# A decoder layer on one core: the experts' up products as three products of rounded parts

## What is computed

```
scores = softmax(xt @ gate_w.T)                     # xt: 2048 x 128, 8 experts
idx = top_k(scores + gate_b, 2);  weights = scores[idx]
for each expert e:                                  # w1[e], w3[e]: 128 x 512, w2[e]: 256 x 128
    h = swiglu((xt @ w1[e] + b1[e]) * (xt @ w3[e] + b3[e]))
    routed += comb[:, e] * (h @ w2[e] + b2[e])      # comb is zero unless e was picked
shared = swiglu((xt @ sw1 + sb1) * (xt @ sw3 + sb3)) @ sw2 + sb2
out = layernorm(xt + routed + shared)
swiglu(x) = min(g, 7) * sigmoid(1.702 * min(g, 7)) * (clip(l, -7, 7) + 1),  g, l = even and odd columns
```

## Time and profile before

| | us |
|---|---|
| runs of the kernel before | 437.20, 444.21, 435.69; median 437.2 |
| the profiled execution, device time | 439.32 |
| its span, first to last instruction | 437.6 |
| attention slots 12 to 46 | 76 to 188 |
| attention slots 47 to 63 | 188 to 246 |
| tiles 0 to 7 with the last chains | 246 to 279 |
| tiles 8 on, with the last routing and padding | 279 to 321 |
| tiles at an even pace | 321 to 406 |
| sums and last norm | 406 to 438 |

### The profile page before, as it was taken

How to read it: one execution, slowest core, us unless ns; L and a number is a source line. 1 busy time by engine, 2 the same in 40 slices (tenths; PEclk the granted TensorE clock), 3 DMA queues, 4 the chain that set the end, 5 groups by cost and what they waited for, 6 DMA issues and landing times.

```text
span 437.6 us, 8506 instructions
## 1 busy us (share of the span) xinstructions
PE 355.7 (81%) x2402; PEld 231.0 (53%) x2415; DVE 280.9 (64%) x834; ACT 175.9 (40%) x498; POOL 192.0 (44%) x377
## 2 busy tenths in 40 slices
PE   2638588878987986987998599887989999999791
PEld 1223356656654764766667455444445555555450
DVE  3424257656877767686876876788566666666422
ACT  1211224433543432334444244434455556555404
POOL 9700014312211366531662344436775666656323
PEclk9999969979988788896989779999999999999896
DMA  4763734575617523130112000102211111110063
GB/s 100 167 184 94 214 90 111 181 225 153 186 66 219 181 81 87 32 103 28 41 52 97 2 18 18 50 13 79 76 54 50 45 44 44 42 45 30 19 199 96
DMA packets 53197, 39.56 MB, mean 90 GB/s; under 512 B 7623, under 2 KB 46632, under 8 KB 53147
## 3 DMA queue, kind: packets, MB, share of 16 engines
q1 hardware_dynamic: 50881, 34.33, 28.1%
q0 software_dynamic: 2272, 4.69, 3.2%
HBM read 26.05 MB, written 12.69 MB: 89 GB/s over the span
## 4 chain that ended last, share of the span: by engine, by line
PE 45%; DVE 23%; issue 8%; DMA 6%; POOL 6%; SPq 5%; ACT 5%; another core or an unknown queue 2%; ACTq 0%; POOLq 0%; DVEq 0%
PE pT L1468 6%; PE pS L1468 6%; PE pM L1479 3%; DVE negmax L921 3%; PE pM L1276 2%; PE pT L1445 2%; PE pT L1300 2%; PE pO L1459 2%; DVE PT L1052 2%; POOL rstd L602 2%; PE pS L1290 2%; PE pO L1313 2%; DMA X<-in_x 2%; PE pS L1469 1%
## 5 line engine op out<-in xcount | busy, mean ns | idle before, releaser
L700 POOL DMA_INDIRECT ys<-sim_rhs,row_dest x39 | 40.7, 1045 | 41.7 <-ACT sim_rhs L855 39.9
L921 DVE TENSOR_REDUCE negmax<-pS 128x4 f32<-128x512 f32 x64 | 43.2, 679 | 19.5 <-PE pS L1290 19.3
L755 ACT ACTIVATE PT<-pT 128x512 f32<-128x512 f32 x64 | 38.1, 595 | 43.9 <-PE pT L1300 43.0
L1290 PE MATMUL pS<-Kdiag,Qst 128*128 128x512 f32 x64 | 42.8, 678 | 13.4 <-DMA Qst<-parts_scr 12.9
L1468 PE MATMUL pT<-W,XH 128*128 (+1 forms) x94 | 51.1, 625 | 0.2 <-issue 0.2
L1468 PE MATMUL pS<-W,XH 128*128 (+1 forms) x94 | 49.0, 603 | 0.0
L1052 DVE TENSOR_TENSOR PT<-pT,PT 128x512 f32<-128x512 f32 x47 | 32.4, 690 | 24.6 <-PE pT L1469 11.4
L600 POOL TENSOR_SCALAR vareps<-meanvar 128x1 f32<-128x1 f32 x32 | 7.3, 227 | 88.9 <-DVE meanvar L950 88.7
L839 ACT COPY XH<-pO 128x384 f32<-128x384 f32 x47 | 22.5, 479 | 48.1 <-PE pO L1461 42.2
L1479 PEld LDWEIGHTS pM<-W,XH 128*128 128x128 f32 x188 | 28.0, 191 | 21.2 <-issue 17.5
L622 POOL DMA_INDIRECT xs<-X,slot x32 | 33.5, 1045 | 8.3 <-issue 6.0
(11 more groups left out here) (264 smaller groups left out, 834.0 us busy)
## 6 DMA issues: line engine op xcount, KB each, us to landing
parts_scr<-qk_hi SPq DMA_DIRECT2D x16, 256.0 KB, 2.9
W<-in_L_ffn_w SPq DMA_DIRECT2D x16, 256.0 KB, 3.2
Kdiag<-parts_scr SPq DMA_DIRECT2D x64, 48.0 KB
Qst<-parts_scr SPq DMA_DIRECT2D x32, 96.0 KB
Kst<-parts_scr SPq DMA_DIRECT2D x32, 96.0 KB
Qdiag<-parts_scr SPq DMA_DIRECT2D x64, 48.0 KB
sim_add<-xs SPq DMA_DIRECT2D x39, 65.0 KB
parts_scr<-qk_lo SPq DMA_DIRECT2D x8, 256.0 KB, 3.4
```

The lines of the kernel that those rows point to most:

```text
L700: pool.indirect_dma_start(ys.ap(), bass.IndirectOffsetOnAxis(ap=row_dest[:, k:k + 1], axis=0), YO[:, i % RING, :], None).then_inc(s_ysc[i ...
L755: act.activation(PT[:, u % 3, :], pT[:, 0, :], ACT.Exp, scale=SCALE).then_inc(p_sb, 1)
L921: dve.tensor_reduce(out=negmax[:, b % 2, HG * j:HG * (j + 1)], in_=pS[:, u % 2, :].rearrange("p (g k) -> p g k", g=HG), axis=AX.X, op=ALU.max,
L1290: pe.matmul(pS[:, u % 2, :], Qst[:, (b // 2) % 2, j, (b % 2) * P:(b % 2 + 1) * P], Kdiag[:, b % 2, j, :, :], start=True, stop=True).then_i ...
```

## The change

The 39 routed tiles no longer multiply float32 operands in the up products. A weight matrix w is split into an upper part rounded to float32r and a lower part, the rest rounded to float32r, and so is x; then x·w is computed as x_hi·w_hi + x_hi·w_lo + x_lo·w_hi, three float32r products. The shared expert's tiles keep float32.

The splitting of the 16 matrices (8 experts, w1 and w3) is a pipeline over slots 12 to 45, two slots a matrix, in four steps: SP loads the raw matrix into one of two buffers (slot 12+2k, after waiting for the store of matrix k-2 to land), ACT copies it rounded into W1 or W3 (next slot, at its end), POOL subtracts in place (the slot after, at its end), SP stores the lower part to a DRAM scratch (the slot after that). When the attention is done with `Kdiag` and `Qdiag`, their place takes the lower parts: 16 loads from the scratch in slots 54, 58, 60 and 64. The down weights come in slots 62 and 66. POOL no longer halves them; instead the row weight is halved, the b2 biases are doubled once (`twice`), and two ACT copies become multiplications by 0.5. In a tile, ACT makes x_hi after its copy to XH, and DVE x_lo between the clips and the gate. `hankel`, `flip`, `x2_of` and one `hidT` move from W1 and W3 to W2. Some semaphores are merged, so that POOL's bias step of slot 10 also waits for the two b_col loads.

```diff
-HALVE_SLOTS = {14: E, **{36 + e: e for e in range(E)}}
-UP_SLOTS = {**{15 + 4 * e: e for e in range(E - 2)}, 62: E - 2, 63: E - 1}
-DOWN_SLOTS = {13 + 4 * k: (2 * k, 2 * k + 1) for k in range(E // 2)}
+SPLIT_LOADS = {54: 0, 58: 1, 60: 2, 64: 3}
+SPLIT_SLOT = 12
+DOWN_SLOTS = {62: range(E // 2), 66: range(E // 2, E)}
...
+    up_scr = nc.dram_tensor("up_scr", (2 * E, P, I2), F32)
...
+        x_hi, x_lo = (t[:, 0, 0, :].rearrange("p (r n) -> p r n", r=2) for t in (Qst, Kst))
+        raw = [sb("raw", [P, I2])[:], W2[:, 3 * G4 * P:4 * G4 * P]]
+        W_lo = [t[:].rearrange("p k j g n -> p (k j g n)") for t in (Kdiag, Qdiag)]
...
+            def raw_weights(k):
+                if k >= 2:
+                    sp.wait_ge(s_w_copy[k % 2], 16 * (k // 2))
+                sp.dma_start(raw[k % 2], (w1, w3)[k // E][k % E]).then_inc(s_w_raw[k % 2], 16)
+
+            def store_lower(k):
+                sp.wait_ge(w_lo, k + 1)
+                sp.dma_start(up_scr.ap()[k], raw[k % 2]).then_inc(s_w_copy[k % 2], 16)
+
+            def load_lower(q):
+
+                sp.wait_ge(s_ps if q < 2 else sT_ps, U * (B - 1 + q % 2))
+                for r in range(2):
+                    sp.wait_ge(s_w_copy[r], 16 * E)
+                for k in range(4 * q, 4 * q + 4):
+                    sp.dma_start(split_of(k)[1].bitcast(F32), up_scr.ap()[k]).then_inc(s_w_lo, 16)
...
-                if n in UP_SLOTS:
-                    if n >= SHARED_SLOT + SHARED_SLOTS * SG:
-                        sp.wait_ge(f_ps, 9 * SG)
-                    up_weights(UP_SLOTS[n], s_w_up if UP_SLOTS[n] < E - 2 else s_w_last)
+                if split_step(n, 0) is not None:
+                    raw_weights(split_step(n, 0))
+                if split_step(n, 3) is not None:
+                    store_lower(split_step(n, 3))
...
-                    pool.tensor_scalar(W2[:, e * I:(e + 1) * I], W2[:, e * I:(e + 1) * I], 0.5, None, ALU.mult).then_inc(w2_half, 1)
+                if split_step(n, 2) is not None:
+                    k = split_step(n, 2)
+                    pool.wait_ge(w_hi, k + 1)
+                    pool.tensor_tensor(raw[k % 2].bitcast(F32R), raw[k % 2], split_of(k)[0].bitcast(F32),
+                                       ALU.subtract).then_inc(w_lo, 1)
...
+                if split_step(n, 1) is not None:
+                    k = split_step(n, 1)
+                    act.wait_ge(s_w_raw[k % 2], 16 * (k // 2 + 1))
+                    act.copy(split_of(k)[0], raw[k % 2]).then_inc(w_hi, 1)
...
                     act.copy(XH[:, p, :], pO[:, 0:3 * P]).then_inc(xh_sb, 1)
+                if NA <= m + 1 < NT:
+                    if m >= NA + 1:
+                        act.wait_ge(b_ps, m)
+                    act.wait_ge(xh_sb, m + 2)
+                    act.copy(x_hi[:, p, :], XH[:, p, 2 * P:3 * P]).then_inc(x_hi_sb, 1)
...
+                r = i + 2
+                if NA <= r < NT:
+                    if r >= NA + 2:
+                        dve.wait_ge(b_ps, r - 1)
+                    dve.wait_ge(x_hi_sb, r - NA + 1)
+                    dve.tensor_tensor(x_lo[:, 1 - p, :], XH[:, 1 - p, 2 * P:3 * P], x_hi[:, 1 - p, :].bitcast(F32),
+                                      ALU.subtract).then_inc(x_lo_sb, 1)
...
-                    pe.matmul(bank, XH[:, 1 - p, 2 * P:3 * P], W[:, bass.ds(e_up * I2, I2)], start=True, stop=False)
+                    if m < NA:
+                        pe.matmul(bank, XH[:, 1 - p, 2 * P:3 * P], (W1_shared, W3_shared)[k][:], start=True, stop=False)
+                    else:
+                        upper, lower = W[:, bass.ds(e_up * I2, I2)], W_lo[k][:, bass.ds(e_up * I2, I2)]
+                        if k == 0:
+                            pe.wait_ge(x_hi_sb, m - NA + 1)
+                        pe.matmul(bank, x_hi[:, 1 - p, :], upper, start=True, stop=False)
+                        pe.matmul(bank, x_hi[:, 1 - p, :], lower, start=False, stop=False)
+                        if k == 0:
+                            pe.wait_ge(x_lo_sb, m - NA + 1)
+                        pe.matmul(bank, x_lo[:, 1 - p, :], upper, start=False, stop=False)
```

More of the change, by code:

```diff
@@ L215, in decoder_layer @@
         hid = sb("hid", [P, 2, I])
-        hidT = [hid[:].rearrange("p k n -> p (k n)"), W1[:, (E - 2) * I2:(E - 1) * I2]]
+        hidT = [hid[:].rearrange("p k n -> p (k n)"), W2[:, 2 * G4 * P:3 * G4 * P]]
         b1_col, b3_col = sb("b1_col", [P, 2, 2]), sb("b3_col", [P, 2, 2])
-        x2_of = [W[:, (E - 1) * I2:E * I2] for W in (W1, W3)]
+        x2_of = [W2[:, g * G4 * P:(g + 1) * G4 * P] for g in range(SG)]
         lin_g, lin_l = XH[:].rearrange("p k n -> p (k n)")[:, 0:G4 * P], PT[:, 3, :]
@@ L358, in x2T, with split_step, split_of @@
             return x2_of[b // G4][:, qcols(b)] if b < G4 * SG else X2T[:, b % 2, :]
+        def split_step(n, step):
+            k, r = divmod(n - SPLIT_SLOT - step, 2)
+            return k if r == 0 and 0 <= k < 2 * E else None
+        def split_of(k):
+            here = slice(k % E * I2, (k % E + 1) * I2)
+            return (W1, W3)[k // E][:, here], W_lo[k // E][:, here]
         def scat_sem(g):
@@ L514, in _ @@
                         sp.dma_start(bias3[3 * k:3 * k + 3, 0:rows * P],
-                                     bias_scr.ap()[:, row:row + rows, :].rearrange("t r n -> t (r n)")).then_inc(s_bias3, 16)
+                                     bias_scr.ap()[:, row:row + rows, :].rearrange("t r n -> t (r n)")).then_inc(s_biasw, 16)
                         row += rows
@@ L570, in _ @@
             pool.memset(batt_inv[:], 0.0).then_inc(c_pad, 1)
-            pool.memset(zero[:], 0.0)
+            pool.memset(twice[:], 2.0).then_inc(c_flip, 1)
+            pool.wait_ge(c_flip, 3)
+            pool.affine_select(out=twice[:], in_=twice[:], compare_op=ALU.is_ge, fill=1.0, base=-2 * BROWS[0], pattern=[[0, 1]],
+                               channel_multiplier=1).then_inc(c_flip, 1)
             pool.memset(bias3[:], 0.0).then_inc(c_bias, 1)
@@ L1443, in shared @@
                     c, step = i // 4, i % 4
-                    first = E * I2 + 2 * c * P + step // 2
-                    pe.matmul(pT[:, 1, :], (W1, W3)[step % 2][:, first:first + 2 * P - step // 2:2], x2_of[g], start=True,
+                    first = 2 * c * P + step // 2
+                    pe.matmul(pT[:, 1, :], (W1_shared, W3_shared)[step % 2][:, first:first + 2 * P - step // 2:2], x2_of[g], start=True,
                               stop=True).then_inc(f_ps, 1)
```

89 lines of the change are left out of this document (44 added, 45 removed).

## The result

| | before | changed |
|---|---|---|
| median of the timed runs, us | 436.4 (434.1 to 444.2, 4 runs) | 446.9 (445.6 to 448.8, 4 runs) |
| the profiled execution's span, us | 437.6 | 447.0 |
| ratio | | 1.026, 95% interval 1.020 to 1.033 |

The changed kernel is slower by about 10 us. The forecast was 433.2 with a range of 424 to 445, so both the time and the sign are missed.

The account below looks back on a forecast made before the run. PE was taken to bound the even tiles and to be near its bound in slots 12 to 46. Profiled 439.3 - 9 (products) + 5 (splitting) + 0 = 435.3, or 433.2 us against the median; range 424 to 445.

Parts of the forecast that it names:

- Part 1, the products: Routed tiles: three float32r products replace each float32 up product, a tile falls from 3.034 to 2.73 us; sum -9 us.
- The loop: Even tiles: the chain through ACT and DVE to hid grows from 2.64 to 2.73 us and sets the tile's pace.
- The rivals of 2.62 and of 3.30 a tile: Routed tiles: PE binds at 2.62, total 426, chance 0.13; float32r product takes 0.33, tile 3.30, total 449, chance 0.08.
- x_lo costs nothing: Routed tiles: DVE's x_lo, 0.29 us, falls into the 0.28 us that DVE waits for tanh, so costed at nothing.
- The tiles before the even pace: The 11 tile intervals before 321 us: half a microsecond gained, since DVE's routing and SP's padding transfers set the pace.
- Part 2, the splitting: Slots 12 to 45: splitting the weights costs +5 us through ACT's in-order waiting, bounds 0 to +19.
- in five of the eight groups: Slots 12 to 45: 1 us lost in each of five of the eight groups of four slots, +5 us.
- a sign of being wrong: Slots 12 to 46: a stage as long as before, or over 125 us, would show the prediction wrong.
- the mechanism of the forecast: Slots 12 to 45: ACT stands at raw loads landing 3.2 us after issue, delaying exponentials and chain copies; waits 1 to 2 us.
- As work this is hidden: Slots 12 to 45: added ACT casts (11 us), POOL subtractions (19 us), stores and loads fit idle time, costing nothing as work.
- The rival of 447 us: Slots 12 to 46: each of 16 raw-matrix waits costs ACT 1.2 us, +19; PE's clock can add; chance 0.11.
- Part 3: Outside the splitting and products: lower-part and down-weight loads in slots 54 to 66, bias doubling, ACT multiplications; cost 0.

Follow-up runs that it names:

- six products in a row: Changed kernel with a routed tile's six float32r products in a row, both bias products behind them, down product last; 449.0 us, 1.023 of before.
- loads ahead: Changed kernel with the cast three slots after the raw load's issue instead of one, subtraction and store four and five after; 435.7 us, 1.003 of before.
- the products alone: Changed kernel with up matrices loaded straight into W1 or W3, without cast, subtraction, or store and load of lower parts; 425.4 us, 0.982 of before.
- the splitting alone: Changed kernel with routed up products single float32 again and no x_hi or x_lo, weight splitting kept; 449.4 us, 1.035 of before.

## Why the prediction was wrong

**Part 1, the products: right in size.** Forecast were 2.73 us a tile and -8.5 for 28; measured 2.757 to 2.775, 28 x 0.277 = -7.8 for the first profile. The reason was half right. I priced each float32r product at 0.22 by itself; it is 0.23, and 0.32 for one behind another type. The products save 0.19 a tile and not 0.42 (which was itself short: I took the second float32 product, 0.91, as 0.86), and 0.09 came from places that I had at nothing. So PE's own part isn't 2.62 but about 2.76. The earlier trace rows had the 0.33 of that case; I put it down to a wait. The loop that I put at 2.73 is real, as the six products in a row show, where it holds most tiles at 2.76: the hand-over of hid takes 0.10 there, and not the 0.05 of the earlier trace rows. That PE and loop come out side by side is chance; the forecast had the loop alone as the bound. The weight load that a rule of the Trainium skill (TensorE: Matmul & The Clock Gate, "What overlaps and what doesn't" in Part 3) adds to each product doesn't show: the products in mid group are 0.23 apart, each with a load of its own. The 0.32 of the first is what the estimate by that rule gave for each; of what its 0.09 is made, no run shows. The rivals of 2.62 and of 3.30 a tile are out, and x_lo costs nothing that shows, as costed.

**The tiles before the even pace: the term was small, the noise large.** With short padding transfers the products give 41.9 - 41.0 = 0.9 us there (-0.5 forecast). The +3.3 of the first profile was neither x_lo nor the products: the padding transfers of the earlier trace rows differ by chip and execution between 8.1 and 11.2 us, and what faster tiles gain ahead of them is spent waiting.

**Part 2, the splitting: the step that failed.** Forecast +5 "in five of the eight groups", bounds 0 to +19. The five profiles with the whole splitting have 128.0 on average, the three without any 110.5: +17.5, near the upper bound, and all five over the 125 us that was named as a sign of being wrong. By the experiments:
- ACT held by raw loads is 127.3 - 122.2 = 5.1 on one chip, 5.8 against the average: the mechanism of the forecast, and its size of 5. The waits were fewer and longer than its 1 to 2 us, up to 4.5, and the one shown took 4.2 us from its issue to ACT's cast, where the forecast had 3.2.
- The sentence "As work this is hidden" failed. The 16 subtractions do lie in POOL's idle time, but while one runs, DVE's operations on SBUF are held to its end, and the chains through DVE are what PE waits for there. With the loads ahead, giving the subtraction to DVE takes 122.2 - 115.7 = 6.5 off; without loads ahead, leaving it out takes 127.3 - 119.3 = 8.0 off. The sum has this term at nothing. Loads ahead without any subtraction wasn't run, so the two terms are known only by these two ways of taking them off.
- 115.7 - 110.5 = 5.2 is left. It isn't waiting: PE is idle 14.4 us with DVE subtracting, and 15.2 to 18.6 in the kernels that split nothing. It is PE's busy time, 101.3 against 90.8 to 95.3, at a granted clock of 0.81 against 0.88 to 0.92. Over the whole +17.5 the same split is 10.6 more idle and 6.8 more busy time. The sum had no term for the clock; the rival of 447 named it. No run shows whether the splitting brings the lower clock about: one execution of the changed kernel had 0.88 like the kernel before, and the four others of the whole splitting 0.81 to 0.83.

So the prediction went wrong by a missing term of 6.5 to 8 us, DVE held by POOL, and a remainder of 5 in which PE ran at a lower clock, not by the mechanism that it named. The rival of 447 us had the right total, with 1.2 us at each of 16 casts as its cause. That mechanism was a third of the loss in the slots; by the totals, beside the same short padding transfers, taking it away gives 1.021 to 1.003, a little under half of the way to the 0.982 of the products alone. Leaving out the subtraction, with ACT's waits at their longest, gives as much, 1.002. That the rival met the total was in good part luck.

**Part 3: 0**, right: slot 46 to tile 0 takes 61.0 to 61.3 with the loads of the lower parts, in both profiles of the changed kernel and with the splitting alone, against 62.1 and 61.8 before.

The sum for the changed kernel, +17.5 in the slots, -7.8 in the tiles and -0.9 ahead of them, is +8.8, against 2.1 to 2.6% of 437, 9 to 11. Where the padding transfers are long, as on those chips, the 0.9 isn't gained; the rest of the gap is within the spread between executions. The best versions measured, with loads ahead and POOL's subtraction in pieces or on DVE, are at 0.993 and 0.988 of the kernel before (the latter's interval reaches 1.001), as the products alone promise 0.982.
